# Attention kernel on one Trainium2 core: the weighing two turns behind the scores, with four buffers of weights

## What is computed

```python
q, k, v = (einsum('bcn,oc->bon', y, W).reshape(b, 8, 64, n) for W in (Wq, Wk, Wv))
attn = softmax(einsum('bhdn,bhdm->bhnm', q, k), axis=-1)
out = x + gamma * merge_heads(einsum('bhnm,bhdm->bnhd', attn, v)) + einsum('bcn,oc->bon', y, Wsc)
```

## Time and profile before

| what | value |
|---|---|
| median of 3 runs | 2943.71 us (2942.43 to 2944.36) |
| the profiled execution's own time | 2940.95 us |
| its span, first to last instruction | 2939.2 us |
| PE busy | 2891.7 us, 98% |
| POOL busy | 2741.2 us, 93% |
| DVE busy | 2016.3 us, 69% |
| ACT busy | 1949.6 us, 66% |
| mean granted clock of TensorE | 0.998 |

### The profile page before, as it was taken

One profiled execution on the slowest core, in us unless ns is written; L12 is line 12 of the kernel. 1 busy time (PEld: TensorE's weight loads), 2 busy tenths in 40 slices (PEclk: granted clock), 3 DMA queues, 4 the chain that ended last, 5 costly groups with the idle time before them and its releaser, 6 DMA issues. The chain is left out here.

```text
span 2939.2 us, 153693 instructions
## 1 busy us (share of the span) xinstructions
PE 2891.7 (98%) x71226; PEld 2434.4 (83%) x71226; DVE 2016.3 (69%) x2665; ACT 1949.6 (66%) x3156; POOL 2741.2 (93%) x2043
## 2 busy tenths in 40 slices
PE   6999999999999999999999999999999999999999
PEld 4787888878888888888878888888888888888776
DVE  7777666666677666666677766666666666666663
ACT  4566676776666677677666667767666666666565
POOL 2799999999999999999999999999999999999998
PEclk9999999999999999999999999999999999999999
DMA  3011110110111011010011101101000000000000
GB/s 138 27 48 29 33 38 23 38 34 17 34 38 56 17 31 41 21 52 18 22 35 48 40 22 38 34 28 45 17 24 17 23 17 23 17 23 17 23 16 19
DMA packets 93090, 94.28 MB, mean 32 GB/s; under 512 B 44320, under 2 KB 90400, under 8 KB 92448
## 3 DMA queue, kind: packets, MB, share of 16 engines
q1 hardware_dynamic: 92448, 84.44, 9.5%
HBM read 56.10 MB, written 18.87 MB: 26 GB/s over the span
## 5 line engine op out<-in xcount | busy, mean ns | idle before, releaser
L985 POOL TENSOR_TENSOR PLO<-PE 128x768 f16<-128x768 f32 x1727 | 2502.8, 1471 | 136.3 <-ACT PE L634 110.3
L794 DVE TENSOR_REDUCE mx<-MX 128x2 f32<-128x768 f32 x1728 | 1657.3, 959 | 863.2 <-PE MX L451 844.2
L634 ACT ACTIVATE PE<-SL 128x768 f32<-128x768 f32 x1728 | 1402.2, 811 | 891.9 <-PE SL L477 882.5
L516 PE MATMUL OB<-V,PE 64*128 64x129 f16 x20736 | 1257.0, 218 | 0.8
L516 PEld LDWEIGHTS OB<-V,PE 64*128 64x128 bf16 x20736 | 1004.6, 94 | 219.7 <-DVE Oe L806 3.3
L477 PE MATMUL SL<-QK 64*128 64x384 f16 x10368 | 1167.5, 323 | 9.8 <-ACT PE L634 9.7
L513 PE MATMUL OB<-V,PLO 64*128 64x65 f16 x20736 | 984.5, 191 | 0.0
L386 PE MATMUL PJ<-X,WT 64*128 64x384 f16 (+2 forms) x7675 | 983.2, 301 | 0.0
L513 PEld LDWEIGHTS OB<-V,PLO 64*128 64x128 f16 x20736 | 741.1, 95 | 0.0
L451 PE MATMUL MX<-QK 64*128 64x384 f16 x3456 | 602.8, 323 | 7.7 <-DVE mx L794 6.1
L477 PEld LDWEIGHTS SL<-QK 64*128 64x128 f16 x10368 | 483.6, 94 | 124.2 <-ACT PE L634 15.9
(11 more groups left out here) (109 smaller groups left out, 986.2 us busy)
## 6 DMA issues: line engine op xcount, KB each, us to landing
gx<-x SPq DMA_DIRECT2D x36, 768.0 KB, 4.6
xr<-x SPq DMA_DIRECT2D x96, 192.0 KB, 2.4
out<-xr SPq DMA_DIRECT2D x96, 192.0 KB, 1.9
X<-x SPq DMA_DIRECT2D x6, 768.0 KB, 8.4
CR<-c SPq DMA_TRANSPOSE x96, 2.4
QK<-wk SPq DMA_DIRECT2D x1, 1024.0 KB, 9.0
QK<-wv SPq DMA_DIRECT2D x1, 1024.0 KB, 11.2
QK<-wq SPq DMA_DIRECT2D x1, 1024.0 KB, 11.9
```

The lines of the kernel that those rows point to most:

```text
L516: last = pe.matmul(acc, upper, v, start=begin, stop=False, skip_group_check=True)
L634: act.activation(PE32[:, s % PB, :].rearrange("p (h n) -> p h n", h=2), SL[:, :, 0:CH], ACT.Exp, scale=1.0 / SS).then_inc(s_exp, 1)
L794: nc.vector.tensor_reduce(mx3[:, n % 2, :, k], MX[:, :, 0:CH], AX.X, ALU.max).then_inc(s_mxf, 1)
L985: nc.gpsimd.tensor_tensor(PLO[:, s % PB, :], PE32[:, s % PB, :], PE32[:, s % PB, :].bitcast(BF16)[:, 1:4 * CH:2], ALU.subtract).then_inc(s ...
```

## The change

Three constants are changed. LAG goes from 3 to 2: part 0 of a weighing stands in turn s + 2, part 1 in turn s + 3. `OB` is emptied in turn 2 instead of 3, and ACT's evacuation, DVE's evacuation and its reciprocal move with it. PB goes from 5 to 4: `exps(s)` waits for the weighing of turn s - 4. The two turns at the seam are now turns 1 and 2, and `THIRDS` gives them the 5 and 13 pieces that turns 2 and 3 had; turn 3 takes turn 1's nine. No instruction is added or removed.

```diff
-PB = 5
+PB = 4
...
-LAG = 3
+LAG = 2
...
-THIRDS = (9, 9, 5, 13, 9, 9, 9, 9, 8, 8, 8, 5, 7, 8, 8, 8, 5, 7)
+THIRDS = (9, 5, 13, 9, 9, 9, 9, 9, 8, 8, 8, 5, 7, 8, 8, 8, 5, 7)
```

## The result

The changed kernel has a median of 2976.49 us (2975.63 to 2978.28, 3 runs) beside 2943.71 before: 1.0117 times, with an interval from 1.0103 to 1.013. By these two medians it is 32.8 us (1.0111 times) slower. The forecast was 2973.5 with a range from 2955 to 2992.

A forecast was written before the change was run, and what follows sets the result against it. PE was taken to set the pace, with POOL close behind. To the profiled 2940.95 us it added 30.3 of waits for POOL and took off 0.5 at the tail: 2970.8, or 2973.5 for the median, range 2955 to 2992.

The forecast's parts named there:

- What bounds the kernel: PE sets the pace at 1.64 us a turn; POOL follows with little room, one split every 1.425 us.
- Part 1: Weighings a turn earlier wait for POOL's late splits in turns 13 and 0: 30.3 us more.
- three terms: Waits for POOL's splits: 8.2 us in 41 key chunks, 4.6 in 3 root-scaling chunks, 15.7 in 18 preparing chunks.
- the carry: A preparation behind split 17 adds an estimated 0.15 us in 12 preparing chunks that follow another: 1.8 us.
- The room by the loads' busy share: LDWEIGHTS at 83% taken as room on PE: 0.28 us a turn, making the key-chunk term 5 us, not 8.2.
- Part 2: Weighing of turn 17 at the seam, evacuations moving along: nothing beyond the 1.8 us, bounded by another 0 to 3.6.
- Part 3: Four buffers: exps(s) wants the weighing of turn s - 4, already ahead of score s on PE; costs nothing.
- Part 4: Start and tail: one weighing leaves the tail, 0.77 us less a 0.24 wait for DVE's split; 0.5 saved.
- that rival: PE's granted clock falls: each preparing or special chunk's wait costs a half-clock turn, 34 us more, 3008 us; chance 0.02.
- Held up once: POOL's lateness paid once, not in each chunk: 2945 us, not slower; chance 0.05 with everything else within 0.2%.
- All short waits hidden: PE hides key chunks' 0.40 us waits; others remain at half size: 10 to 16 us, 2953 to 2959; chance 0.09.
- Nothing absorbed: Waits on PE paid in full and lateness carries over: 40 to 55 us, 2984 to 2999 us; chance 0.15.

The follow-up runs named there:

- the repair: The changed kernel with DVE's first statistics of a chunk in turn 2 instead of 1, behind the accumulator's emptying: 2972.73 us, 1.0103.
- b_lag3_pb4: Four buffers at three turns (PB = 4, LAG = 3, the old THIRDS): 3368.4 us in a single run.
- a_pb5: The changed kernel with five buffers of weights instead of four, still at LAG = 2: 2976.4 us, 1.0116.
- l_less3: Three turns and five buffers, as in the kernel before, with POOL's extra operations left nearly out (8 columns instead of 384): 2940.29 us, 0.9993.
- d_keys_dve: The changed kernel with the lower half of the keys' differences on DVE instead of POOL: 3018.39 us, 1.0257.
- h_dve: The changed kernel with the keys' lower halves and the next batch's preparation on DVE, and the statistics in turn 2: 3011.1 us, 1.0233.

## Why the prediction was right

*What bounds the kernel*, and POOL's pace of 1.425 us: right. The key chunk grew to 29.77 where 29.7 was forecast.

*Part 1*, the two rows laid side by side: right in the size of its three terms, 28.4 us measured where 28.5 stood before the carry. That a wait is absorbed by 0.15 to 0.20 was an estimate. In chunk 14 it held, 0.40 of lateness and 0.18 lost in turn 13; over the 41 key chunks, with loads that waited 0.27 to 0.32, turns 13 and 14 together lost 0.19 to 0.24. Without it the sum would have been 40.2, 12 us too many. The handoff of 0.05 was right in all three places. Where the time is lost was right for the key chunks alone. The forecast had one payment of 0.87 at turn 0 behind each preparing chunk; there came 0.19 in turns 13 and 14 and 0.64 at turn 0. It had one of 1.54 in turn 13 of each special chunk; there came 0.64 in turn 11 and 0.97 in turns 13 and 14. The sums fit because POOL catches up while PE stands still, so that a first wait shortens the second; the prediction had used this only for its lower bound. That the two terms fit so closely is in part luck. The carry of 1.8 was not there: each group of extras starts clean, as the same part had argued.

*The room by the loads' busy share*, 0.28 us a turn, by which the key chunks would lose 5 us in all instead of 8.2: the traces measured 8.8, so it overstates the room that a wait can use. (It rested on the Trainium skill, "Perfetto Trace Analysis", section "Identifying the Most-Contended Engine"; the measurement decides.) The room was where the gap between two loads showed it, 0.13 of the 0.31 in chunk 14.

*Part 2* is the step that failed: "the weighing behind them waits for the same chain". On ACT that held. On DVE the emptying moved by a turn and past nothing, but toward the statistics of turn 1, which didn't move. I had listed the work that moves and not the work that it moves up to. It cost 4.7 us by the traces, 3.8 by the repair. The prediction's own sign of being wrong, that chunks without key units grow too, came true here: nine chunks with statistics, no key units and nothing to prepare grew by 0.24 to 0.29 (one by 0.55). Of its other signs, L516's waits for POOL came to 83 and not over 100, with the 36.1 us that it asked for.

*Part 3*, buffers at nothing: right, and `b_lag3_pb4` shows that the cover is PE's order.

*Part 4*: the last weighing starts 2.89 us behind the last score's start instead of 3.42, which is the 0.53 forecast. But the profiled tail was only 0.2 shorter. The three transposes at the end took 0.87 us instead of 0.52. These are the rows before and after, and the window after:

```profile
2935.68 0.52 PE L434 MATMUL PJ<-identf,attn 128*128 128x128 f32 x3 [2.02 <-DVE attn L847]
```

```profile
2970.01 0.87 PE L434 MATMUL PJ<-identf,attn 128*128 128x128 f32 x3 [2.02 <-DVE attn L847]
```

```profile
2970.00:2971.50 1.50, 0.87 (x3) 0.48 (x3) 0.51 (x1) 0.00 (x0) 0.00 (x0) 0.50 0.00 0
```

The granted clock was 0.50, 1.2 GHz, behind 2.02 us in which PE waited for DVE's division. The Trainium skill, "TensorE: Matmul & The Clock Gate", Part 1, says that an idle PE falls to half rate, and this row agrees. But the same wait of 2.02 us stands in all 14 traces of this case: in nine, the kernel before and `a_pb5` among them, the transposes took 0.52, and in five, `l_less3` at three turns among them, 0.87 or 0.88. So it is not the change that costs this 0.35 us, and which of the two a run gets is left open. With 0.52, as in `a_pb5`, the stretch from the last score's start is 9.41 us instead of 9.95, the 0.5 that was forecast. In the three stretches around the waits above the clock stayed at 1.00, so that rival fell. The prediction called its waits shorter than the one of the window 329 to 331, which was 1.17 us at the load; its own 1.74 was not, but the longest that came was 1.05.

*The sum.* The trace grew by 34.7 us where 29.8 was forecast, 5 too few: 4.7 for the statistics and 2 for the start, tail and single turns, less the 1.8 of the carry. The median came only 3.0 over the forecast because the three runs before had a median of 2943.7, above the 2942.1 to 2942.5 of all later groups; that part is luck.

*The other rivals.* Held up once: no, POOL goes idle 567 times and each chunk pays anew. All short waits hidden: no, chunk 14 paid 0.18 of its 0.40 in turn 13 and the others much the same. Nothing absorbed: no. What remains open are single turns 0.3 to 0.4 us longer in a few chunks, about 1 us together, which I didn't follow.

## What to carry to other kernels

The slack of a software pipeline is found without building the shorter one: lay the end of the producer's operation beside the start of the consumer's previous one, chunk kind by chunk kind, add the handoff, and take off what the gap before the next wait and the lead of the loads give. Do so for every turn of the chunk, since an early wait takes from a later one. An engine's share of 93% says nothing of this; the clumping of its extra operations does, and moving one of them, with the ACT operation that feeds it, a turn earlier brought back 13 us. When a step moves, list also what it moves up against on each queue: here a 0.55 us operation that stood still cost more than the tail gave.

## What the runs showed of the hardware

A DVE `tensor_tensor` of 128x384 with both inputs in SBUF took 1.47 to 1.79 us in 90 places while POOL was splitting, though the last split of the kernel, twice as wide and with POOL idle, takes DVE 0.95 us. This is `d_keys_dve` by line and then the preparation's operation in `h_dve` (durations min/median/max):

```profile
L794 DVE TENSOR_TENSOR QK<-DF,QK x90: 1469/1565/1790, 110.3 to 2747.1; 128x384 f16<-128x384 f32 x90
```

```profile
L965 DVE TENSOR_TENSOR X<-gx,X x72: 546/996/1785, 383.3 to 2105.7; 128x384 f16<-128x384 f32 x72
```

In all 90 places of the first, and in 54 of the second's 72, a split was running when DVE's operation began, and the operation ended 0.41 to 0.42 us behind that split's end, however long the split still had to go. In the other 18 the operation began in the last 0.14 us of a split and took 0.55 us, which is then its own length; the split that followed it took 1.78 to 1.81 us instead of 1.47.

The Trainium skill, "SBUF — State Buffer", section "SBUF: two separate sides", says that DVE and GpSimd share a port pair which one of them holds for a whole instruction, and that this holds for a DVE operation with two inputs in SBUF too, against a GpSimd operation that reads SBUF, as the split does. The rows agree: neither was slowed a little, each stood until the other had ended. DVE's L806, which has one of its two inputs in PSUM, took 0.54 to 0.56 us and ran beside POOL's splits untouched.
